# Expert stores of an MoE layer ordered by expert instead of one behind the other, and the first tile's rows transposed earlier

## The reference

```
scores = xf @ gate_w.T ;  ew, ei = top_k(scores, 2)        # two of eight experts per token
routed = sum over the two experts e of ew * down_e( silu(gate_e x) * up_e x )
shared = silu(xf @ sh_gate) * (xf @ sh_up) @ sh_down       # all tokens
h = h + routed + sigmoid(xf @ se_gate) * shared
```

## Time and profile before

| | |
|---|---|
| median of 3 runs | 1591.97 us (1591.94 to 1593.3) |
| the profiled execution | 1593.97 us, its span 1592.2 us |
| PE busy | 1389.7 us, 87% of the span |
| DVE, ACT, POOL busy | 833.2, 373.7, 480.7 us |
| expert part of ffn0 | from about 404 us to the last store's landing at 655 us |
| expert part of ffn1 | from about 1285 us to the end |

### The profile page before, as it was taken

One profiled execution on the slowest core, in us unless ns is written; L12 is line 12 of the kernel. 1 busy time (PEld: TensorE's weight loads), 2 busy tenths in 40 slices (PEclk: granted clock), 3 DMA queues, 4 the chain that ended last, 5 costly groups with the idle time before them and its releaser, 6 DMA issues.

```text
span 1592.2 us, 20911 instructions
## 1 busy us (share of the span) xinstructions
PE 1389.7 (87%) x6461; PEld 1077.6 (68%) x6462; DVE 833.2 (52%) x1711; ACT 373.7 (23%) x711; POOL 480.7 (30%) x350
## 2 busy tenths in 40 slices
PE   0585739999899999289999899999999979989996
PEld 0583317888444444137776688888888869879885
DVE  8875597655222222563667765555555533323332
ACT  1113114221111111232222312332333212212221
POOL 0662430351244443001211035433332111333441
PEclk9999779999999999689999999999999999999998
DMA  4492005102955554600000404666666588666553
GB/s 97 92 162 32 0 21 179 61 21 68 344 95 94 93 94 66 196 21 0 1 0 1 140 21 133 219 214 219 207 214 207 215 312 276 178 181 179 92 86 40
DMA packets 87387, 193.95 MB, mean 122 GB/s; under 512 B 28657, under 2 KB 32753, under 8 KB 83825
## 3 DMA queue, kind: packets, MB, share of 16 engines
q1 hardware_dynamic: 67232, 151.18, 29.4%
q0 software_dynamic: 20096, 42.02, 14.7%
HBM read 112.24 MB, written 77.87 MB: 119 GB/s over the span
## 4 chain that ended last, share of the span: by engine, by line
PE 62%; DMA 20%; DVE 11%; issue 4%; ACT 1%; POOL 0%; SPq 0%; POOLq 0%; DVEq 0%; ACTq 0%
PE ps L1507 22%; PE ps L1567 19%; DMA h_rows<-moe_scratch 7%; DMA h_rows<-held,moe_scratch 6%; PE ps L2029 6%; PE ps L429 4%; DMA out<-held,moe_scratch 3%; DVE held L482 2%; DMA out<-moe_scratch 2%; PE ps L538 1%; PE ps L2001 1%; PE ps L778 1%; PE ps L779 1%; PE ps L2054 1%; PE ps L1601 1%
## 5 line engine op out<-in xcount | busy, mean ns | idle before, releaser
L1567 PE MATMUL ps<-moe_rounded 128*128 128x384 f32 (+2 forms) x1800 | 374.1, 350 | 0.0
L1567 PEld LDWEIGHTS ps<-moe_rounded 128*128 128x128 f32 x1800 | 325.7, 188 | 32.9
L1277 DVE SCALAR_TENSOR_TENSOR held<-ps,moe_scratch,held 128x512 f32<-128x512 f32 (+1 forms) x255 | 187.4, 747 | 179.1 <-PE ps L1507 178.9
L1507 PE MATMUL ps<-moe_expert_parts,moe_rows_parts 128*128 (+1 forms) x1320 | 258.3, 348 | 4.7 <-DVE moe_rows_parts L1285 3.2
L1507 PE MATMUL ps<-moe_rounded 128*128 128x512 f32 (+3 forms) x885 | 239.2, 390 | 7.7 <-DVE moe_rounded L1259 5.7
L1507 PEld LDWEIGHTS ps<-moe_expert_parts,moe_rows_parts 128*128 128x128 f32 (+1 forms) x1320 | 218.7, 189 | 18.1 <-issue 5.4
L1507 PEld LDWEIGHTS ps<-moe_rounded 128*128 128x128 f32 (+2 forms) x885 | 145.4, 170 | 45.8 <-DVE moe_rounded L1259 8.1
L1291 DVE TENSOR_TENSOR moe_scratch<-moe_scratch,ps 128x256 f32<-128x256 f32 (+1 forms) x80 | 37.7, 471 | 230.2 <-ACT moe_scratch L1488 230.2
L1628 PE MATMUL ps<-moe_experts,moe_scratch 128*128 x320 | 145.9, 599 | 1.7 <-ACT moe_scratch L1474 1.1
L1383 POOL TENSOR_TENSOR moe_split_parts<-moe_scratch,moe_split_parts 128x704 fp32r<-128x704 f32 (+2 forms) x48 | 88.7, 1854 | 172.7 <-ACT moe_split_parts L1463 172.6
L1367 POOL DMA_INDIRECT slot_tokens<-moe_scratch x68 | 73.6, 1082 | 168.5 <-DVE held L1277 161.5
(11 more groups left out here) (305 smaller groups left out, 1679.2 us busy)
## 6 DMA issues: line engine op xcount, KB each, us to landing
moe_expert_parts<-expert_parts SPq DMA_DIRECT2D x8, 3840.0 KB, 14.7
expert_parts<-moe_split_parts SPq DMA_DIRECT2D x32, 704.0 KB, 3.7
moe_scratch<-in_ffn_gate_up SPq DMA_DIRECT2D x32, 352.0 KB, 5.0
xn_rows<-moe_xn SPq DMA_DIRECT2D x2, 4096.0 KB, 12.8
moe_experts<-in_ffn_gate_up SPq DMA_DIRECT2D x8, 1024.0 KB, 12.6
expert_parts<-moe_split_parts SPq DMA_DIRECT2D x8, 1024.0 KB, 4.7
moe_scratch<-in_ffn_sh_gate_up SPq DMA_DIRECT2D x15, 512.0 KB, 3.5
tokens<-sb SPq DMA_DIRECT2D x16, 256.0 KB, 4.5
```

The lines of the kernel that those rows point to most:

```text
L1277: v.scalar_tensor_tensor(out=hb[0:rows, t, :], in0=ps[0:rows, ADDED[t % 3], :], scalar=sg[0:rows, t:t + 1], in1=hb[0:rows, t, :], op0=ALU. ...
L1507: mm = t.matmul(out, lhs(k, x), rhs(k, y), start=(k == 0 and i == 0), stop=(k == ks - 1 and i == 2))
L1567: mm = t.matmul(unit_banks(u, m)[j], weights(k, x, j), xT[y][:, k, unit_cols(m)], start=(k == 0 and i == 0), stop=(k == KD - 1 and i == 2))
```

## The change

1. **Stores by expert.** A store waits only for the stores of the tiles that lie before its own expert's first tile. DVE works out this number (`behind`) and, for each of four semaphores, the value to wait for (`landed`), in the new `others_behind`, at the head of `tile_slots` and `tile_experts`. POOL reads four values from SBUF for each store. There are four semaphores of stores instead of two, and the spare rows become 4 x 128, so that unfilled slots of four neighbouring tiles don't meet. The initial stores of the spare rows become 128x4x512 instead of 128x512.
2. **First gathers.** The gather of tile 2 waits for the first piece of the stored stream (counted on `xs`) instead of all five.
3. **First tile earlier.** PE transposes the rows of tile 0 in front of the last shared down products, into bank 6; ACT and DVE copy them out in the last block, ahead of "hi" and "lo" of the last unit. The wait for all sums (`acc`) stands behind the first gate and up products instead of ahead of the transposes.

```diff
+        def others_behind():
+            c.link(v.tensor_tensor(cmp, bc(iot.unsqueeze(2), 2, NE), bc(incl.unsqueeze(1), 1, NTILE), ALU.is_ge))
+            c.link(v.tensor_tensor(cmp, cmp, bc(incl.unsqueeze(1), 1, NTILE), ALU.mult))
+            c.link(v.tensor_reduce(behind, cmp[:, :, 0:NE - 1], AX.X, ALU.max))
+            for x in range(DEEP):
+                c.put(v.tensor_scalar(landed[:, x], behind, float(DEEP - 1 - x), None, ALU.add))
+            c.wait()
+            c.link(v.tensor_scalar(landed, landed, 2, None, ALU.logical_shift_right))
+            c.link(v.tensor_scalar(landed, landed, 16.0, float(Y0), ALU.mult, ALU.add))
...
         def block(b, u):
             for what, m in DVE_STEPS:
+                if split_w and is_last(b) and (what, m) == ("lo", NU - 1):
+                    rows_lo(0, 0)
...
                 elif t == 2:
-                    p.wait_ge(hst, 16 * (NQ + 1))
+                    p.wait_ge(xs, 5 * 16)
...
+                if o == 0:
+                    p.wait_ge(hst, 16 * NQ)
+                before_it = [p.value_load(landed[0:1, x, o:o + 1], min_val=Y0, max_val=Y0 + 16 * (NTILE // DEEP)) for x in range(DEEP)]
                 p.wait_ge(eyr, o + 1)
-                if o:
-                    p.wait_ge(yst[1 - o % 2], 16 * ((o + 1) // 2))
-                else:
-                    p.wait_ge(hst, 16 * (NQ + 1))
+                for x in range(DEEP):
+                    p.wait_ge(yst[x], before_it[x])
                 p.indirect_dma_start(out=hd, ...
-                                     in_=ey_of[o % DEEP], in_offset=None, compute_op=ALU.add).then_inc(yst[o % 2], 16)
+                                     in_=ey_of[o % DEEP], in_offset=None, compute_op=ALU.add).then_inc(yst[o % DEEP], 16)
...
             for what, m in ACT_STEPS:
+                if is_last(b) and (what, m) == ("hi", NU - 1):
+                    s.wait_ge(hidr, b * NU + NU - 1)
+                    if split_w:
+                        s.wait_ge(plr, NE * CHUNKS)
+                    rows_turned(0, 0)
...
         blocks(t, block)
+        turn_rows(0, 0)
         for tile in UNITS[NU - 1]:
             down(NSH - 1, (NSH - 1) % 2, NU - 1, tile)
...
-        t.wait_ge(acc, NSH * T)
         if split_w:
             t.sem_inc(ed, 1)
-        turn_rows(0, 0)
         gate_up(0, 0, expert_of(0))
+        t.wait_ge(acc, NSH * T)
         turn_rows(1, 1)
```

More of the change, by code:

```diff
@@ L844, in ffn_layer @@
         r = Arena(g.rows_parts, 0)
-        xgT, ehT = r.take(2, 2, KD, P), r.take(2, 2, NF, P)
+        ehT, xgT = r.take(2, 2, NF, P), r.take(2, 2, KD, P)
         b = Arena(g.high, g.rows_at + ROWS, g.high_at)
@@ L866, in ffn_layer @@
     eti, esl = a.take(NTILE, dt=I32), a.take(NTILE, dt=I32)
+    behind, landed = a.take(NTILE), a.take(DEEP, NTILE, dt=U32)
     a.at = max(a.at, g.high_at + GLA_HIGH)
@@ L897, in ffn_layer @@
     ed, eyr = sem(name + "_e_down"), sem(name + "_e_out_ready")
-    yst = [sem(f"{name}_e_out_stored{u}") for u in range(2)]
+    yst, Y0 = g.rows_stored, 16 + G0
+    SCATS = 2 * T if split_w else 2 * T - DEEP
     hst = sem(name + "_h_stored")
@@ L981, in sync @@
         shared(1)
-        sp.dma_start(xd[SPARE:, :], xn[:, 0, :]).then_inc(xs, 16)
-        sp.dma_start(hd[SPARE:, :], xn[:, 0, :]).then_inc(xs, 16)
+        for rows in (xd, hd):
+            sp.dma_start(rows[SPARE:, :].rearrange("(k p) d -> p k d", p=P), xn[:, 0:DEEP, :]).then_inc(xs, 16)
         sp.wait_ge(xs, 4 * 16)
@@ L992, in slots_in @@
         def slots_in():
-            sp.wait_ge(scat, 2 * T * 16)
+            sp.wait_ge(scat, SCATS * 16)
+            for x in range(2 * T - SCATS):
+                sp.wait_ge(yst[x], 16)
             sp.dma_start(idx_u, slots.rearrange("(p t) o -> p t o", t=NTILE)).then_inc(ix, 16)
@@ L1052, in stored @@
     def stored(sp):
[L1054 to L1057, removed]
+        for x in range(DEEP):
+            sp.wait_ge(yst[x], Y0 + 16 * (NTILE // DEEP))
+        sp.wait_ge(xs, 5 * 16)
+        sp.wait_ge(hst, 16 * NQ)
     def blocks(eng, body):
@@ L1330, in vector, with rows_bank @@
         out_rows(NTILE - 1, (NTILE - 1) % DEEP)
+    def rows_bank(t):
+        return RANK_BANK if isinstance(t, int) and t == 0 else ADDED[0]
     def halves(t):
@@ L1467, in scalar @@
         blocks(s, block)
-        def rows_turned(t, u):
-            s.wait_ge(tx, t + 1)
-            if not early(t):
-                s.wait_ge(eg, t - 1)
-            to = xgT[:, u, 0] if split_w else xgT[:, u]
-            s.activation(to.rearrange("p k n -> p (k n)"), ps[:, 4, :], ACT.Copy).then_inc(txr, 1)
         def hidden_hi(t, u):
@@ L1588, in down @@
                            lambda k, p: whl[:, u, p, SGW:], 1).then_inc(dn, 1)
-        blocks(t, block)
-        for tile in UNITS[NU - 1]:
-            down(NSH - 1, (NSH - 1) % 2, NU - 1, tile)
         def turn_rows(n, x):
@@ L1600, in turn_rows @@
             for k in range(KD):
-                ins = t.transpose(ps[:, 4, k * P:(k + 1) * P], xg_of[x][:, k * P:(k + 1) * P], ident)
+                ins = t.transpose(ps[:, rows_bank(n), k * P:(k + 1) * P], xg_of[x][:, k * P:(k + 1) * P], ident)
             ins.then_inc(tx, 1)
+        blocks(t, block)
+        turn_rows(0, 0)
+        for tile in UNITS[NU - 1]:
+            down(NSH - 1, (NSH - 1) % 2, NU - 1, tile)
         def expert_of(n):
@@ L2151, in __init__ @@
         self.rows_gathered = [sem(f"rows_gathered{k}") for k in range(DEEP)]
+        self.rows_stored = [sem(f"last_slots_then_e_out_stored{k}") for k in range(DEEP)]
     def look_through(self, nc, base):
```

33 lines of the change are left out of this document (20 added, 13 removed).

## The result

The changed kernel took 1575.26 us (median of 4 runs, 1573.01 to 1577.51), the kernel before 1592.63 (4 runs, 1591.94 to 1595.16): a ratio of 0.9891, 95% interval 0.9876 to 0.9906, so 17.4 us faster, or 15.0 to 19.7. The predicted 1576.5 is 1.2 us off and inside the interval. The profiled execution took 1577.39 us for a span of 1575.6; before it was 1592.2, so the trace has 16.6 us to explain.

The account below looks back on a forecast made before the run. PE was taken to set the time, the chain of stores costing only where PE waits or a part ends. The terms summed to -15.5 us, from the median of 1591.97 to 1576.5 us, range 1570.5 to 1587.

Parts of the forecast that it names:

- Late gather: ffn1, gather awaited until 1411.97: the 6.46 us stall goes and the clock stays up (-2.2), together -8.7 us.
- gather of tile 2: Start of ffn1's experts: issued once the first piece is ready, ahead of the weight loads, -2.9 us.
- end of ffn1: Last store of ffn1 follows its output by 0.27 us, at 1580.4 instead of 1582.41: -2.0 us.
- The gather's own term: Start of ffn1's experts: the -2.9 us for the gather of tile 2, added to the sum.
- First tile: Start of experts in both parts: first product earlier, -1.4 us in ffn1 and -1.4 in ffn0, clock -1.8 in ffn0.
- fast loads: Rival, start of experts: first loads take 0.3 us, 2.3 us more gained, 1574; counted inside the forecast's 0.70.
- The clock term: ffn0, first expert product: clock kept with less idle time, 3.60 instead of 5.39 us, -1.8 us.
- Routing: First blocks, nine DVE instructions: +2.7 us of wait in ffn1, +1.1 for its clock, +1.6 in ffn0.
- End of ffn0: Last store of ffn0 begins at 644.0 instead of 647.96 but runs beside weight loads: -2.7 us.
- POOL's loads: POOL, every tile: four loads at 0.6 us make 5.6 us, just fitting PE's 5.81, cost 0.
- The rivals of 0.9 and 1.05 us a load: POOL's loads slower, PE losing time in ffn0: at 0.9 us 1586.5, chance 0.10; at 1.05 us 1606.5, chance 0.06.

Follow-up runs that it names:

- Experiment 1: Changed kernel with the gather of tile 2 behind the whole stream again and the first tile's rows turned behind the sums as before; 1582.21 us, ratio 0.9929.
- experiment 2: Kernel before, with only the gather of tile 2 released by the first piece of the stream; 1591.77 us, ratio 0.9996.
- experiment 3: Kernel before, with only the first tile's transposes, copies and wait for the sums moved as in the change; 1595.67 us, ratio 1.0014.
- experiment 10: Kernel before with the early gather of tile 2 and the first tile's move, stores still by tile; 1592.68 us, ratio 0.9999.
- Experiment 4: Changed kernel without the first tile's move; 1581.56 us, ratio 0.9931 to the kernel before.
- experiment 5: Changed kernel run and profiled once more, nothing altered; 1572.96 us, ratio 0.989 to the kernel before.
- experiment 6: Changed kernel with the nine routing instructions on DVE moved behind the last "lo" of the first block; 1570.05 us, ratio 0.9868 to the kernel before.
- experiment 7: Kernel of experiment 6 with the copies of the first tile's rows also moved behind "hi" and "lo"; 1568.39 us, ratio 0.9854 to the kernel before.
- experiment 8: Changed kernel with each of the four loads per store on POOL made twice; 1587.71 us, ratio 0.9975 to the kernel before.
- experiment 9: Changed kernel with the gather of tile 2 waiting for the whole stream again, first tile's move kept; 1584.8 us, ratio 0.9951 to the kernel before.

## Why the prediction was right

The forecast's mechanism and its sum held: -15.5 against -16.6 of span. By its own steps:

- **Late gather (-8.7), gather of tile 2 (-2.9) and end of ffn1 (-2.0)**: together -13.6, and the trace has -15.7 between the second product of ffn1 and the last store. The first two came as reckoned, 11.6, the end gave 1.8; 1.8 more came from the small "issue" waits of PE, which the prediction didn't have. Experiment 1 has the late wait gone by the stores alone. The reason given, that a gather is issued in time once its store needn't wait, is borne out by experiments 2, 3 and 10, which all keep the stores by tile and all have late waits of 4.3 us or more for gathers, while no kernel with the stores by expert has one. Which tile it hits varies: 1382, 1413, 1449 or 1450 us.
- **The gather's own term** failed as one that adds. In experiments 2 and 4 it was worth nothing, with the move it is worth 9.7 us. The step "-2.9" read a wait's length in a row and left out what would come next: a chain of stores that gives it back, or a slow product that runs in the same time.
- **First tile (-1.4, -1.4, clock -1.8)**: -4.6 where -6.5 was measured, given the early gather. Experiment 4 and the changed kernel in experiment 5 show the parts: the second product of ffn0 at 413.50 and 411.62, -1.9, or -2.1 counted from their first waits at 272.40 and 272.66; in ffn1, where both are traced from the wait for routing on (930.13 and 927.23), the second product at 1299.17 and 1292.41, -6.8 less the -2.9 of before, -3.9, of which 1.5 are the slower clock of one execution. So each start gave 2.1 to 2.4 us, more than 1.4, because the loads cost 0 in ffn0 and 0.55 us in ffn1 (the rival "fast loads" was nearer). The clock term has its size in the two profiles (5.39 to 3.70 us) but not its reason: experiments 1 and 4 have the idle time and keep the clock, and of the four kernels with the old start it fell in the two without the routing and the loads, the one before and experiment 2. What decides it stays open.
- **Routing (+2.7, +1.1, +1.6)**: 2.60 us more wait in ffn1, 1.14 in ffn0, and the clock took 0.6 on each of two groups and 0.4 on a third (1.57, 1.53 and 1.24 us instead of 0.96, 0.89 and 0.85): 1.6 us. That is 5.3 to 5.4 against 5.4. The waits are the routing's: experiment 6 took both back. The clock's 1.6 can't be put down to the longer wait alone: three of the six executions with the short wait (experiments 2, 7 and 10) lost 1.6 us there as well. Of the time experiment 6 gave 2.9 us.
- **End of ffn0 (-2.7)**: the landing was 4.3 us earlier in all, of which the start of ffn0 gave 1.9, so the end 2.4. The store began 5.9 us sooner and took 1.56 us longer beside the weight loads, as weighed.
- **POOL's loads (0)**: right, and with more room than reckoned: 3.31 us a tile, not 5.6. The rivals of 0.9 and 1.05 us a load priced a load as if nothing ran beside it. By the Trainium skill (DMA: Bandwidth & Descriptors, Latency and other measured facts) a `tensor_load` would take at least some 600 ns; 159 on POOL in ffn0 had a median of 287 ns, below that floor, though 30 of them, one per tile from 438.9 us on, took 529 to 979. Loads can cost, but elsewhere: experiment 8 paid for twice the loads not through gathers but through the late stores at the end of ffn0.
- **Not foreseen**: some 3 us of lower clock at the start of ffn1's experts (4.33 + 5.68 instead of 3.05 + 4.1), which is in the profiled execution and not in experiment 5. And 1.5 us came behind the last store, which began 15.1 us sooner for a span 16.6 shorter. The clock's +3 stands against these -1.5, the -1.8 of the small waits and the -2 by which the first tile's move gave more than reckoned: the parts of the sum were less exact than the sum.

That the prediction came within 1.2 us is thus partly luck: with the change undone in parts, its additive terms miss by 2 us in experiment 2, by 7 in experiment 3 (-4.6 reckoned, +2.2 measured), and by 7 in experiment 9 (0.9908 by the changed kernel's ratio and the gather's 2.9, 0.9951 measured). For the stores alone, experiment 1, the terms give 8.0 us (8.7 + 2.0 + 2.7 less 5.4) and 11.3 were measured.

## What to carry over

Two edits that each shorten the way to the same wait must be priced together: shifting PE forward moves it into the next late transfer, and releasing that transfer is worth nothing while PE isn't there yet; here, with the stores by expert in, one alone cost some 3 us (at the edge of the noise), the other gave 0, both gave 6. First take away what hands the gain back (here the chain of stores), then look at the starts. And put bookkeeping on an engine at the first place where it is not waited for, rather than beside the bookkeeping that it resembles: nine small instructions two units later took 3.7 us of waiting away in the trace, and 2.9 us between medians whose intervals overlap.

## What the runs showed of the hardware

- POOL's sequencer works on register loads while its DMA instructions ahead of them run: four loads of 0.54 us pitch left 0.14 us more from gather to gather (3.31 against 3.17), the next four 2.7.
- TensorE's clock does not follow from the idle time alone. Behind 4.34 or 4.35 us of waiting in ffn1's first block the next three products took 1.33 to 1.65 us in all six executions with the routing there (five kernels; 0.96 at full clock), and 0.96 behind the 1.74 to 1.77 us of six others, but in three of these six (experiments 2, 7 and 10) the clock fell 1 to 2 us later and cost 1.6 us after all. At the start of ffn1's experts, behind 1.97 or 1.98 us, the 12 down products took 3.05 us in one execution of the changed kernel and 4.33 in another, 4.61 in experiments 3 and 6, and 3.03 to 3.06 in experiments 8, 9 and 10; behind 1.70 us, in the four kernels without the move, 3.04 to 3.06.
- Four transposes took 1.11 or 1.12 us behind every wait of 3.4 us or more for a gather that is shown here, and 0.66 behind those of 2.85, 2.88 and 0.32 us.
- A short TENSOR_LOAD from SBUF took 0.29 us on POOL in the median, but in ffn0 one of the four per tile took 0.53 to 0.98 (30 of 159).
